# A recommender forward pass on one core: one table picked by TensorE for all samples, first-layer sums in halves

## What is computed

```python
emb = vmap(lambda tab, idx: tab[idx])(tables, cat_features)      # 26 x 512 x 128
linear_output = emb.sum(over tables) + relu(numerical @ w_wide + b_wide)
x = concatenate([numerical, emb of all tables], axis=1)          # 512 x (13 + 26*128)
x = relu(x @ W1 + b1)                                            # 512 x 256
x = relu(x @ W2 + b2)                                            # 512 x 128
return sigmoid(x @ W3 + b3 + linear_output)                      # 512 x 128
```

## Time and profile before

| | us |
|---|---|
| median of 3 runs | 248.84 (247.80 to 249.22) |
| the profiled execution, its own time | 247.35 |
| its span | 245.5 |
| TensorE busy | 110.2 |
| GpSimd busy (99 gathers) | 95.0 |
| VectorE busy | 37.7 |
| ScalarE busy | 21.0 |
| mean granted TensorE clock | 0.79 |

### The profile page before, as it was taken

One profiled execution on the slowest core, in us unless ns is written; L12 is line 12 of the kernel. 1 busy time (PEld: TensorE's weight loads), 2 busy tenths in 40 slices (PEclk: granted clock), 3 DMA queues, 4 the chain that ended last, 5 costly groups with the idle time before them and its releaser, 6 DMA issues.

```text
span 245.5 us, 2014 instructions
## 1 busy us (share of the span) xinstructions
PE 110.2 (45%) x398; PEld 67.5 (28%) x398; DVE 37.7 (15%) x106; ACT 21.0 (9%) x45; POOL 95.0 (39%) x108
## 2 busy tenths in 40 slices
PE   2657004500700004500009059979799991007795
PEld 0143001300300001300004026545466660005594
DVE  2031001000100002000001023244244430001132
ACT  0100000000000000000000001011011120001242
POOL 5777777777777777777750000000000000000000
PEclk9999999955695555875555759999999997555999
DMA  6994315444443353433231012131000000000001
GB/s 189 297 234 100 58 50 89 62 51 50 103 56 51 58 46 95 57 50 54 54 54 43 0 47 72 62 87 52 8 3 4 4 1 3 1 2 0 0 13 32
DMA packets 11163, 14.05 MB, mean 57 GB/s; under 512 B 3196, under 2 KB 8031, under 8 KB 11151
## 3 DMA queue, kind: packets, MB, share of 16 engines
q0 software_dynamic: 3168, 6.49, 17.7%
q10 hardware_dynamic: 3359, 3.63, 5.1%
q1 hardware_dynamic: 4624, 3.80, 5.1%
HBM read 13.65 MB, written 0.26 MB: 57 GB/s over the span
## 4 chain that ended last, share of the span: by engine, by line
SPq 54%; issue 35%; PE 8%; DMA 1%; ACT 1%; DVE 1%; ACTq 0%; DVEq 0%
SPq L229 48%; SPq L224 6%; PE first_layer L335 2%; PE first_layer L378 2%; PE mlp L401 1%; DMA first_cat<-in_r_cat_features 1%; ACT emb_t L559 1%; PE turn L320 1%; DMA emb<-in_L_rec_tables 0%; PE total L409 0%; PE turn L369 0%; PE total L395 0%; PE first_layer L351 0%; PE total L390 0%; ACT late_t L572 0%
## 5 line engine op out<-in xcount | busy, mean ns | idle before, releaser
L335 PE MATMUL first_layer<-emb_t,w 128*128 128x512 f32 (+3 forms) x104 | 58.2, 692 | 104.2 <-issue 90.3
L270 POOL DMA_INDIRECT emb<-in_L_rec_tables,row_idx x98 | 92.5, 944 | 30.0 <-issue 29.5
L335 PEld LDWEIGHTS first_layer<-emb_t,w 128*128 128x128 f32 x104 | 21.9, 231 | 124.4 <-issue 106.2
L500 DVE TENSOR_TENSOR emb_sum<-turn,emb_sum 128x512 f32<-128x512 f32 (+3 forms) x25 | 16.0, 638 | 182.0 <-issue 106.4
L559 ACT COPY emb_t<-turn 128x512 f32<-128x512 f32 (+3 forms) x26 | 14.1, 544 | 207.5 <-PE turn L320 75.8
L320 PE MATMUL turn<-ident,emb 128*128 128x128 f32 x94 | 17.6, 314 | 20.7 <-DMA emb<-in_L_rec_tables 18.1
L344 PE MATMUL total<-hot,block_rows 128*128 128x256 f32 (+1 forms) x98 | 25.0, 386 | 0.0
L320 PEld LDWEIGHTS turn<-ident,emb 128*128 128x128 f32 x94 | 14.3, 166 | 36.1 <-issue 35.8
L344 PEld LDWEIGHTS total<-hot,block_rows 128*128 128x128 f32 (+1 forms) x98 | 17.8, 199 | 1.6
L486 DVE TENSOR_SCALAR hot<-pick_row,row_no 128x256 f32<-128x256 f32 x49 | 14.8, 352 | 0.0
L378 PE MATMUL first_layer<-late_t,w 128*128 128x128 f32 x32 | 5.4, 291 | 0.6 <-ACT late_t L572 0.4
(11 more groups left out here) (51 smaller groups left out, 28.9 us busy)
## 6 DMA issues: line engine op xcount, KB each, us to landing
emb<-in_L_rec_tables SPq DMA_DIRECT2D x256, 0.5 KB
block_rows<-in_L_rec_tables ACTq DMA_DIRECT2D x12, 256.0 KB, 2.8
w<-in_L_rec_W SPq DMA_DIRECT2D x2, 1152.0 KB
emb<-in_L_rec_tables ACTq DMA_DIRECT2D x128, 0.5 KB
emb<-in_L_rec_tables,row_idx POOLq DMA_INDIRECT x98
w<-in_L_rec_W SPq DMA_DIRECT2D x1, 768.0 KB, 5.2
w<-in_L_rec_W SPq DMA_DIRECT2D x1, 256.0 KB
out<-y SPq DMA_DIRECT2D x4, 64.0 KB, 1.6
```

What stands on the lines that cost most here:

```text
L270: nc.gpsimd.indirect_dma_start(emb[:, t, c, :], None, rows, bass.IndirectOffsetOnAxis(ap=index, axis=0)).then_inc(landed, 16)
L335: mm = nc.tensor.matmul(first_layer[k][:, cols], w1[:, t, chunk(k)], emb_t[:, i % SLOTS, cols], start=False, stop=False, skip_group_check= ...
L500: nc.vector.tensor_tensor(emb_sum[:, cols], turn[i % 2][:, cols], emb_sum[:, cols], ALU.add).then_inc(added, 1)
```

## The change

- **Picked table.** `PICK_TABLE` is 12 instead of 22, and all four of its tiles are picked: `hot` and the moving operand of the picking matmuls have 512 columns instead of 256. 49 blocks as before, spread over 36 parts instead of 20.
- **Gathers.** 97 instead of 99, the first included. The tiles fetched by SP and ScalarE are the same three.
- **Parts.** Every part is half a table, 256 columns, with chunks 0 and 2 (q = 0) or 1 and 3 (q = 1). There are 46. Table 0 stands as (0,0),(0,2) at place 36 and as (0,1),(0,3) at place 43. The late tables are 23 and 24; table 25 comes last in the body.
- **Banks.** The first layer has four banks, one for each half of W1 and each q, so chunks 0 and 2 lie in other banks than 1 and 3. Layer 2 writes into the unused half of these banks; `mlp` is gone.
- **Order.** TensorE turns part i + 1 before the picked blocks and the product of part i. The ring of copies has six places instead of four. The last product of the body comes behind the first late turn.
- **ScalarE** issues four rows after each copy instead of eight.
- **Tail.** VectorE adds each turned late tile to `emb_sum` (`add_tile`); the sum of late tiles and its matmul are gone. The products of chunks 2 and 3 wait for `h2_ready` of two chunks earlier. Layer 2 of chunk 2 stands behind the last late product.

```diff
-SLOTS = 4
+LATE_TABLES = (23, 24)
+SLOTS = 6
-ROWS_A_STEP = 8
-PICK_TABLE = 22
-PICK_FROM = 2
+ROWS_A_STEP = 4
+PICK_TABLE = 12
...
+    OTHERS = [t for t in range(1, T) if t not in LATE_TABLES and t != PICK_TABLE]
+    PARTS = [(t, q) for t in OTHERS[:-4] for q in range(2)] + [(0, 0)]
+    PARTS += [(t, q) for t in OTHERS[-4:-1] for q in range(2)] + [(0, 1)]
+    PARTS += [(t, q) for t in OTHERS[-1:] for q in range(2)]
...
-    PICK_PARTS = (2, LAST - 4)
-    PICK_END = LAST - 3
+    PICK_PARTS = (2, LAST - 8)
+    PICK_END = LAST - 7
+
+    def tiles(i):
+        t, q = PARTS[i]
+        return [(t, q + 2 * j) for j in range(HALF)]
...
+        def first_half(k, q):
+            return first_layer[k][q][:, 0:HW]
+
+        def first_chunk(k, c):
+            return first_layer[k][c % 2][:, chunk(c // 2)]
+
+        def second_chunk(c):
+            return first_layer[0][c % 2][:, HW + c // 2 * P:HW + (c // 2 + 1) * P]
+
+        def by_halves(ap):
+            return ap.rearrange("x (j q p) -> x q j p", j=HALF, q=2)
...
-        first_layer = [bank(f"first_layer{k}") for k in range(KH)]
+        first_layer = [[bank(f"first_layer{k}_{q}") for q in range(2)] for k in range(KH)]
...
             def sum_part(i):
-                t, lo, hi = PARTS[i]
-                cols = slice(lo * P, hi * P)
+                t, q = PARTS[i]
                 wait_w1(t)
                 pe.wait_ge(copied, i + 1)
                 for k in range(KH):
-                    mm = nc.tensor.matmul(first_layer[k][:, cols], w1[:, t, chunk(k)], emb_t[:, i % SLOTS, cols],
+                    mm = nc.tensor.matmul(first_half(k, q), w1[:, t, chunk(k)], emb_t[:, i % SLOTS, :],
...
             def sum_picked():
                 pe.wait_ge(pick_copied, 1)
-                for k in range(KH):
-                    nc.tensor.matmul(first_layer[k][:, PC:B], w1[:, PICK_TABLE, chunk(k)], pick_t[:, :],
-                                     start=False, stop=False, skip_group_check=True)
-
+                wait_w1(PICK_TABLE)
+                for q in range(2):
+                    for k in range(KH):
+                        nc.tensor.matmul(first_half(k, q), w1[:, PICK_TABLE, chunk(k)], by_halves(pick_t[:, :])[:, q, :, :],
+                                         start=False, stop=False, skip_group_check=True)
+
+            turn_part(0)
             for i in range(LAST):
-                turn_part(i)
+                if i + 1 < LAST:
+                    turn_part(i + 1)
                 for j in blocks(i):
                     pick_block(j)
-                sum_part(i)
+                if i + 1 < LAST:
+                    sum_part(i)
                 if i == PICK_END:
                     sum_picked()
...
                 if n < 2:
                     pe.wait_ge(added, LAST - 1 + n)
                 else:
-                    pe.wait_ge(late_copied, n - 1)
+                    pe.wait_ge(late_added, n - 1)
...
             def begin_total(c):
...
+                pe.wait_ge(late_added, (c + 1) * LATE)
...
             for c in range(CH):
                 n = c * LATE
                 turn_tile(n)
-                if c >= 1:
-                    add_late(c - 1)
+                if c == 0:
+                    sum_part(LAST - 1)
+                else:
+                    sum_tile(n - 1)
+                    begin_total(c - 1)
+                if c >= 2:
+                    layer3(c - 2)
+                turn_tile(n + 1)
+                sum_tile(n)
+                if 1 <= c < CH - 1:
                     layer2(c - 1)
-                sum_tile(n)
-                turn_tile(n + 1)
-                begin_total(c)
-                if c >= 1:
-                    layer3(c - 1)
-                sum_tile(n + 1)
-            add_late(CH - 1)
+            sum_tile(TILES - 1)
+            layer2(CH - 2)
             layer2(CH - 1)
+            layer3(CH - 2)
+            begin_total(CH - 1)
             layer3(CH - 1)
```

More of the change, by code:

```diff
@@ L66, in rows_apart @@
         return (t, c) in BY_SYNC + BY_SCALAR
-    BODY_TILES = [(0, 0)] + [(t, c) for t, lo, hi in PARTS for c in range(lo, hi) if (t, c) != (0, 0) and not rows_apart(t, c)]
+    BODY_TILES = [(0, 0)] + [tile for i in range(LAST) for tile in tiles(i) if tile != (0, 0) and not rows_apart(*tile)]
     def part_of(t, c):
-        return next(i for i, (u, lo, hi) in enumerate(PARTS) if u == t and lo <= c < hi)
+        return PARTS.index((t, c % 2))
     def by_pool(i):
-        t, lo, hi = PARTS[i]
-        return sum(not rows_apart(t, c) for c in range(lo, hi))
+        return sum(not rows_apart(t, c) for t, c in tiles(i))
     rows = tables.rearrange("t v d -> (t v) d")
@@ L282, in _ @@
                 c, g = divmod(n, LATE)
-                gather(BODY + g, c, column(BODY + g, c), late_gathered[n])
+                gather(LATE_TABLES[g], c, column(LATE_TABLES[g], c), late_gathered[n])
         @block.tensor
@@ L316, in turn_part @@
                     pe.wait_ge(added, i - 1)
-                for c in range(lo, hi):
+                for j, (t, c) in enumerate(tiles(i)):
                     if (t, c) in fetched:
                         pe.wait_ge(fetched[t, c], 16 * P)
-                    mm = nc.tensor.transpose(turn[i % 2][:, chunk(c)], emb[:, t, c, :], ident[:, :])
+                    mm = nc.tensor.transpose(turn[i % 2][:, chunk(j)], emb[:, t, c, :], ident[:, :])
                 mm.then_inc(turned, 1)
@@ L367, in turn_tile @@
                 else:
-                    pe.wait_ge(late_copied, n - 1)
-                nc.tensor.transpose(turn[n % 2][:, 0:P], emb[:, BODY + g, c, :], ident[:, :]
+                    pe.wait_ge(late_added, n - 1)
+                nc.tensor.transpose(late_turn(n), emb[:, LATE_TABLES[g], c, :], ident[:, :]
                                     ).then_inc(late_turned, 1)
@@ L374, in sum_tile @@
                 pe.wait_ge(late_copied, n + 1)
[L375 to L378, removed]
+                if c >= 2:
+                    pe.wait_ge(h2_ready, c - 1)
+                for k, done in enumerate([h1_low_done, h1_high_done]):
+                    mm = nc.tensor.matmul(first_chunk(k, c), w1[:, LATE_TABLES[g], chunk(k)], late_t[:, n, :],
                                           start=False, stop=False, skip_group_check=True)
@@ L490, in _ @@
                 hot_block(j)
-            for i, (_, lo, hi) in enumerate(PARTS):
-                cols = slice(lo * P, hi * P)
+            for i, (_, q) in enumerate(PARTS):
                 dve.wait_ge(copied, i + 1)
-                if i == 0:
-                    nc.vector.tensor_copy(emb_sum[:, :], turn[0][:, :]).then_inc(added, 1)
+                if i < 2:
+                    nc.vector.tensor_copy(emb_sum[:, q, :], turn[i][:, 0:HW]).then_inc(added, 1)
                 else:
@@ L553, in _ @@
             regs = []
-            for i, (_, lo, hi) in enumerate(PARTS):
-                cols = slice(lo * P, hi * P)
+            for i in range(LAST):
                 act.wait_ge(turned, i + 1)
@@ L558, in _ @@
                     act.wait_ge(used, i - SLOTS + 1)
-                nc.scalar.copy(emb_t[:, i % SLOTS, cols], turn[i % 2][:, cols]).then_inc(copied, 1)
+                nc.scalar.copy(emb_t[:, i % SLOTS, :], turn[i % 2][:, 0:HW]).then_inc(copied, 1)
                 if i == PICK_PARTS[1] - 1:
                     act.wait_ge(hot_used, BLOCKS)
-                    nc.scalar.copy(pick_t[:, :], pick_bank[:, 0:PW]).then_inc(pick_copied, 1)
+                    nc.scalar.copy(pick_t[:, :], pick_bank[:, :]).then_inc(pick_copied, 1)
                 if i < PIECES:
```

123 lines of the change are left out of this document (63 added, 60 removed).

## The result

The changed kernel takes 237.24 us (median of 4 runs, 235.59 to 237.31); the kernel before, run beside it, 248.47 us. The ratio is 0.9531, 95% interval 0.9501 to 0.956: faster by 4.7%. The forecast was 240.7 us, with a range of 236 to 246. The profiled execution took 237.23 us with a span of 235.3 us; the sum had said 237.4.

What follows compares the result with a forecast made beforehand. Bound: instruction issue, slowed by GpSimd's gathers, and TensorE's wait for SP's rows. Landing 219.2 + 3.2 + 9.6 + 4.2 + 1.2 = 237.4 span, 8.1 less than before; 248.84 - 8.1 = 240.7 us, range 236 to 246.

Steps and rivals of the forecast that it cites:

- Bound, and the slow stretch: Until GpSimd's gathers are worked off, every sequencer passes one traced instruction per 1.4 us; ends at 140.05, 2.8 us sooner.
- Halves and blocks: TensorE's products, turns and picked blocks from 140.05: 74.0 us plus 2.3 at low clock, reaching tile (0,3) at 216.4.
- the wait: TensorE idle for embedding tile (0,3), fetched by SP row by row: 18.1 us before, about 3 forecast.
- SP: SP's row fetches for tile (0,3): everything behind moves by -2.5 us, last row issued at 218.0, landed at 219.2.
- Turning ahead: Turning each half before the previous product hides ScalarE's copies and offset loads; three loads of 1.75, 5 us as cover.
- The tail: After the last row lands: 3.2 us to the first late turn, 9.6 of late chunks, 4.2 of activations and store.
- the late chunks: The four late chunks in the tail, 10.3 us before, were to take 9.6 including the last product.
- The clock in the tail: TensorE's clock may drop after its wait for (0,3), costing 0 or 2.3 us; 1.2 taken.
- TensorE late: Rival, 0.15: TensorE reaches the wait for (0,3) at 220 to 226; at 224 the time is 244.3 us.
- Loads out from under the shorter products: Rival: weight loads show at 256-column products after 140 us, giving 252.2 us; 0.09 together with a longer slow stretch.
- The shorter slow stretch: Rival, 0.09: half as many rows per ScalarE burst could save 3 us of the slow stretch; 237 to 238 us.
- The slow stretch not being set by the number of gathers: Rival, 0.09: the slow stretch ends at 142.9 whatever the gathers, row and end 2.5 us later; 243.2 us.

Runs made afterwards that it cites:

- the memsets: Changed kernel with a GpSimd memset behind every fourth gather (176.63 us) or every eighth (161.43 and 161.91 us).

## Why the prediction was right

*Bound, and the slow stretch.* Right. Its end was put at 140.05 and lies at 140.2; the count of 1.405 us a gather held with 98, 96 and 88 gathers behind the first, for ends at 142.86, 140.2 and 128.8. What the prediction did not know is that this stretch goes with the chip: one chip had it in both of its sets, two others in none, with the same programs. What makes it stays open. The prediction's words "until GpSimd's gathers are worked off" can't mean their transfers. In the kernel before, GpSimd's DMA queue moves its last packets between 128 and 130 us,

```profile
q0 software_dynamic: 32, 0.07, 24.0%
```

and none after, but the slow pace lasts to 142.86; in the changed kernel the last ones come before 127, and it lasts to 140.2. A backlog of something else that each gather leaves behind would fit; the memsets were to test it and did not reach a chip with the stretch. One rival was not tested at all: the pace is one per *traced* instruction, and every run here was recorded, so no run can tell a limit of the chip from one of the recording. How many gathers would be best on a chip that has the stretch stays open too.

*Halves and blocks.* Right. TensorE was to stand at the product of part 7 at 140; that is the product at 140.70, the eighth. It was to reach the wait at 216.4 and did at 218.1: it began 0.65 us later than the forecast switch, and the work took 75.1 us and not 74.0 (the same counts at 0.86 and 0.22 give 74.6, so half of this was rounding down). The low clock cost what was said: it lasted from the product at 140.70 to 145.3, 4.6 us. The wait was to be about 3 us, under 5, and is 1.5.

*SP.* Right: landing at 219.2 foretold, 219.56 measured.

*Turning ahead.* Its sum was right, but its weight was told too low. The prediction took it as cover for ScalarE's loads ("5 us") and as 3 us of the tail, and let the idle time of TensorE carry the change. The runs without it come out within 1% of before: 8 to 11 us hang on it, because TensorE has only 1.5 us to spare. The five halves without blocks ahead of the wait for (0,3), 0.73 us each, were missing from my price. So the gain is not TensorE's filled waiting in itself; filling it was free only because the turns were moved ahead in the same change.

*The tail.* The first part was right to 0.1 us: 3.2 us from the landing to the first late turn. The term that failed is the late chunks, "9.6": from 222.80 to 230.68 they took 7.9. I had subtracted from the kernel before only what was taken out. The pieces of the chain before and after show the rest. Before, in each late chunk:

```profile
235.54 0.62 PE first_layer L378 x4
...
236.50 0.61 PE mlp L401 x4
```

After:

```profile
225.45 0.45 PE first_layer L403 x4
225.90 0.45 PE first_layer L418 x4
```

Four passes that took 0.62 behind a wait take 0.45 without it. In three chunks with two such places that is 1.0 us, and layer 2 of chunk 2 (0.45) stands behind the late products now; 1.5 of the 1.7 missing. That the parted banks did this was not tried by itself. The end behind was 4.6 instead of 4.2: the 0.45 of that layer 2 only moved there.

*The clock in the tail.* I took 1.2 between 0 and 2.3; it was 0, the granted clock is 1.00 from 219.60 to the end. Behind the wait of 1.5 us the clock stayed up; behind the one of 3.4 us (the run with eight gathers less) TensorE worked at half of it. The sum of the misses is +0.4 (landing) - 1.7 + 0.4 - 1.2 = -2.1 us, which is 237.4 against 235.3.

*From the span to the time.* The forecast of 240.7 is 3.5 us over the measured 237.24, and only 2.1 of them are in the span. The rest is the base: I took the 8.1 us off the median of before, 248.84, but that kernel's profiled execution was 1.5 us quicker than its median, while that of the changed kernel is its median. That the forecast lies 3.5 us off and not more is partly luck: the late landing and the longer end made up 0.8 us of what the late chunks and the clock had too much.

*The rivals.* TensorE late: not here, but exactly this happens when the turns go behind. Loads out from under the shorter products: no; 256-column products take 0.86 us from start to start with a load under each pass, 0.215, half of the 0.43 of 512 columns. The Trainium skill's sentence that load and matmul both set the spacing (TensorE: Matmul & The Clock Gate, section Back-to-back issue gap) changes nothing at this width, by this row. The shorter slow stretch: no, it ends where the count of gathers puts it although ScalarE's bursts are half as long; its time, 237 to 238, was also worked out wrongly, as an end at 236 is 239.3 on the base used elsewhere. The slow stretch not being set by the number of gathers: no, by the two kernels with gathers left out. On what disturbs SP's issue, the Trainium skill (DMA: Bandwidth & Descriptors, section SWDGE vs HWDGE vs iDMA) calls DMAs issued by SP and ScalarE immune to the interference with GpSimd's descriptor rings. Read widely, as in that rival, the trace of the slow chip differs (0.70 us an issue); on the quick chip it agrees, 0.23 us an issue beside running gathers.

*Two readings.* Between 142.86 and 144.41 the chain of before has five rows, not six; nothing in the sum hangs on it. And SP's steps don't double "whenever" ScalarE bursts: beside the burst from 95.6 to 104.3 single steps reach 1.40 us, but their median stays at 0.7.

## What to carry to other kernels

Price a shift of work by the slack of whoever receives it: here the change filled 18 us of waiting with picking, and what decided whether that paid was a reordering of one line that kept TensorE from losing some 10 us at 0.7 to 2.0 us apiece. When several engines show one odd pace, count instructions: a constant per instruction found on three engines let the end of a 140 us stretch be forecast to 0.2 us. And compare on the same chip; a kernel tuned on one kind of chip has another bound on the other.

## What the runs showed that was not expected

The same program takes 248 us on one chip and 142 on two others. What the traces of the changed kernel show to differ is a stretch in which SP, ScalarE and TensorE get one traced instruction through in 1.40 us each (700 ns median for SP's issue, against 228). It lasts 1.405 us for each of GpSimd's gathers, and so ends some 13 to 14 us after their last packet. The change gains on both kinds, ratios 0.953 and 0.969, but not in the same places: on the slow one 2.1 us lie before the last row of SP and 8 us behind it; on the quick one two gathers less are 2.5 us at 1.25 us each, and for the other 2 us there is no trace of the kernel before to say where. A kernel with every tile gathered, which the slow chip's numbers make look best (205 to 210 us by an estimate from the rows, not tried there), is about 2% slower than before on the quick ones.
